# Seven block products for eight in the gate product of a quantised FFN kernel, with weight sums in natural layout and a one-step rounding

## The chip, the cores and the metric

The kernel runs on one core of one Trainium2 chip. The metric is the device time of one execution in microseconds (us), taken as the median of several runs; lower is better.

## What is computed

The reference is a cross attention followed by a quantised gated feed-forward layer, both with a residual. Cut to what matters:

```python
x = x + xattn(layernorm(x), ctx, Wq, Wkv)          # x: 2 x 2048 x 512, ctx: 2 x 128 x 512
h = act_qdq(layernorm(x))                          # rounded to multiples of one scale, 16 bits
up   = act_qdq(h @ lpbq_dequant(w_up).T)           # 512 -> 1536
gate = act_qdq(h @ lpbq_dequant(w_gate).T)         # 512 -> 1536
sig  = fixed_qdq_u16(sigmoid(gate))
gate = act_qdq(gate * sig)
o    = act_qdq(gate * up)
x = x + o @ lpbq_dequant(w_down).T                 # 1536 -> 512
```

act_qdq takes its scale from the largest absolute value of the whole tensor, so each of these steps needs a maximum over all 4096 tokens before the next can be scaled. lpbq_dequant rounds the weights to 4 bits in blocks of 32, with one scale a block.

## The kernel before

The 4096 tokens are eight groups of 512. The 1536 rows of the gate and up weights are six units of 256 a group, 48 units in all. Integers and weights are too wide for fp16, so each is held as a high and a low fp16 part, and a product of two such values is three matmuls (high x high, low x high, high x low). One unit is 2 halves x 4 slices of the 512 inputs x 3 = 24 matmuls of 128x128 on 128x512 (lines 864 to 873), and its result, 128x1024 f32, lies in two PSUM banks. Unit n takes banks 0, 1 or 2, 3 in turn, so it waits for g_ev, the copy of unit n-2 out of PSUM (line 877).

The stages follow each other, because of the maxima:

- Attention and the quantisation of the gate weights. GpSimd quantises the weights in 24 parts of 768 elements (quant_weights, lines 685 to 697): multiply by the inverse scale, add ROUND, subtract ROUND, multiply by the scale. Eight parts belong to the gate, eight to the up, eight to the down weights. GpSimd also takes each maximum across partitions (all_max, line 683).
- The gate product (L871). ScalarE copies each unit from PSUM into one of two buffers gate_out (take_gate, L993), writes its signs (L1138) and, for later groups, rounds tokens to integers (h_int, L1106). VectorE takes the unit's maximum (L1478) and splits the turned tokens into high and low (split_h, L1467, L1469). SyncE stores the unit in DRAM (gate_park, line 434), then the signs (line 436), then issues the turns (DMA transposes) of the tokens of a later group (turn_half, line 421). All DMAs of this stage stand in SyncE's one queue, in the order of the program. The order is written out by hand: a function a unit, with extra work tied to unit numbers. ScalarE's copy of unit n waits until the store of unit n-2 has landed (g_st), since both use the same gate_out.
- The up weights are loaded at line 403 and the down weights at line 443 into the same buffer WN. They are split into two fp16 parts (natural_hi, natural_lo, L1396) and turned by DMA (lines 407 and 411).
- The up product (L903), whose units rotate over four bank pairs, while ScalarE and VectorE compute the sigmoid and gate product from gate tiles that are fetched again; six gate tiles were kept on chip.
- A first pass of the down product with raw values (L929), while VectorE finds the maximum of the product o; then the down product itself (L948, L975).

In the stage of attention TensorE turns the gate weights by matmul (turn_weights), and their parts lie in WG.

## Time and profile before

| | |
|---|---|
| median of 3 runs | 902.86 us (901.2 to 903.91) |
| profiled execution: span from first to last instruction | 898.3 us |
| profiled execution: own time | not recorded apart from its span; the runs above are other executions |
| gate product, first to last matmul | 130.1 to 380.6 us |
| up product | 380.6 to 631.8 us |
| first pass of the down product | 640.0 to 726.2 us |
| down product | 728.6 to 895.1 us |

The page is one profiled execution. An engine's share says how long it had an instruction in work, and an average over stages with different limits hides which engine a stage waits for; so the stages above are read one by one. PE is TensorE, PEld its weight load, DVE VectorE, ACT ScalarE, POOL GpSimd, SPq SyncE's queue of DMA issues. PEclk is the granted clock of TensorE as a share of full speed.

### The profile page before, as it was taken

To read this page: it belongs to the slowest core of one execution; us is meant where nothing else is said; L and a number is where in the kernel's file an instruction comes from. 1 tells how busy PE (TensorE), PEld (TensorE's weight loads), DVE (VectorE), ACT (ScalarE), POOL (GpSimd) and SP (SyncE) were. 2 spreads that over 40 slices of the span, in tenths; PEclk is the share of its full clock that TensorE was granted. 3 is DMA by queue.
4 is the path that set the end of the run, shared out by engine and by line. 5 is a ranking of instruction groups with operands and counts; after the bars stand their busy time and mean duration, and the time that the engine had idled before them with its cause. 6 is when DMAs were issued, how large, how long until landed. Compare 5 with 4: busy or idle time off the path is not lost.

```text
span 898.3 us, 11791 instructions
## 1 busy us (share of the span) xinstructions
PE 865.5 (96%) x4144; PEld 426.7 (47%) x4144; DVE 651.1 (72%) x918; ACT 560.2 (62%) x673; POOL 157.4 (18%) x160
## 2 busy tenths in 40 slices
PE   7999969999999999999999989999799989999998
PEld 5777544444444444444444434444344434444443
DVE  4879883754346243279997859856999997999892
ACT  2378875553553454489997859763789975555430
POOL 0099940089001950000000000000000000000000
PEclk9999989999999999999999999999999999999999
DMA  9822319775369649884339993799998897989872
GB/s 347 332 93 98 128 59 305 205 194 198 140 234 296 206 161 294 322 319 157 132 149 327 363 347 142 251 402 373 374 379 265 276 322 271 386 286 406 317 294 100
DMA packets 107548, 230.20 MB, mean 256 GB/s; under 512 B 47216, under 2 KB 47216, under 8 KB 105328
## 3 DMA queue, kind: packets, MB, share of 16 engines
q1 hardware_dynamic: 106352, 225.48, 70.8%
q10 hardware_dynamic: 1152, 4.19, 1.3%
q8 instruction: 21, 0.34, 0.2%
q14 instruction: 23, 0.19, 0.1%
HBM read 127.40 MB, written 92.27 MB: 245 GB/s over the span
## 4 chain that ended last, share of the span: by engine, by line
PE 66%; DVE 16%; issue 8%; DMA 6%; ACT 3%; SPq 0%; POOL 0%; DVEq 0%; ACTq 0%
PE ps L871 28%; PE ps L948 13%; PE ps L903 10%; PE ps L975 3%; DVE big L1596 3%; PE ps L804 3%; DVE big L1589 3%; PE ps L743 2%; PE ps L818 2%; DVE small L1523 2%; DMA big<-gate_park 2%; DMA product_park<-big 2%; DVE small L1511 2%; DVE big L1518 1%; PE ps L965 1%
## 5 line engine op out<-in xcount | busy, mean ns | idle before, releaser
L993 ACT ACTIVATE big<-ps 128x1024 f32<-128x1024 f32 (+2 forms) x166 | 138.7, 845 | 189.6 <-PE ps L871 102.8
L871 PE MATMUL ps<-big 128*128 (+1 forms) x1152 | 250.5, 381 | 2.3 <-DVE big L1460 2.3
L903 PE MATMUL ps<-big 128*128 (+1 forms) x1152 | 249.0, 379 | 2.3 <-ACT big L993 2.3
L871 PEld LDWEIGHTS ps<-big 128*128 128x128 f16 x1152 | 113.1, 98 | 139.4 <-issue 4.6
L903 PEld LDWEIGHTS ps<-big 128*128 128x128 f16 x1152 | 112.6, 98 | 138.5 <-issue 2.8
L1478 DVE TENSOR_REDUCE small<-big 128x1 f32<-128x1024 f32 x48 | 58.3, 1219 | 135.2 <-ACT big L993 135.1
L948 PE MATMUL ps<-big 128*128 128x512 f16 x576 | 125.1, 379 | 2.7 <-DVE big L1617 2.7
L683 POOL PARTITION_ALL_REDUCE small<-small x8 | 3.3, 410 | 509.3 <-DVE small L1558 181.5
L948 PEld LDWEIGHTS ps<-big 128*128 128x128 f16 x576 | 56.2, 98 | 71.1 <-issue 2.9
L929 PE MATMUL ps<-big 128*128 128x512 f16 x384 | 85.2, 383 | 4.5 <-ACT big L1223 4.5
L1529 DVE CUSTOM_DVE_ANT_0 big<-big,small 128x1024 f32<-128x1024 int16 x48 | 61.7, 1284 | 7.3 <-ACT big L1173 0.5
L1252 ACT ACTIVATE big<-big,small 128x1024 int16<-128x1024 f32 x48 | 53.2, 1136 | 16.7 <-DMA big<-up_park 16.5
L929 PEld LDWEIGHTS ps<-big 128*128 128x128 f16 x384 | 37.4, 99 | 52.0 <-issue 5.5
L1511 DVE TENSOR_REDUCE small<-big 128x1 f32<-128x1024 f32 x48 | 58.0, 1214 | 3.4 <-ACT big L993 3.4
L1258 ACT ACTIVATE big<-big 128x1024 f16<-128x1024 int16 x24 | 25.3, 1055 | 53.0 <-DVE big L1611 53.0
L1181 ACT ACTIVATE big<-big,small 128x1024 f32<-128x1024 int16 x48 | 55.1, 1149 | 4.6 <-ACT big L1173 0.4
L1173 ACT ACTIVATE big<-big,small 128x1024 int16<-128x1024 f32 x48 | 54.5, 1136 | 2.4 <-DMA big<-gate_park 2.4
L1216 ACT ACTIVATE big<-big,small 128x1024 int16<-128x1024 f32 x48 | 52.3, 1135 | 5.7 <-DVE small L1444 2.9
L1138 ACT ACTIVATE big<-big 128x1024 int16<-128x1024 f32 x48 | 50.5, 1052 | 6.9 <-DMA sign_park<-big 5.9
L743 PE MATMUL ps<-small,big 128*128 128x128 f32 x248 | 37.9, 294 | 12.8 <-DVE big L1389 5.1
L743 PEld LDWEIGHTS ps<-small,big 128*128 128x128 f32 x248 | 32.2, 153 | 28.6 <-issue 18.4
L691 POOL TENSOR_TENSOR big<-big,small 128x768 f32<-128x768 f32 x24 | 36.5, 1521 | 22.0 <-issue 21.6
(101 smaller groups left out, 1008.9 us busy)
## 6 DMA issues: line engine op xcount, KB each, us to landing
big<-up_park SPq DMA_DIRECT2D x90, 512.0 KB, 6.5
up_park<-big SPq DMA_DIRECT2D x48, 512.0 KB, 3.9
gate_park<-big SPq DMA_DIRECT2D x42, 512.0 KB, 2.9
big<-gate_park SPq DMA_DIRECT2D x42, 512.0 KB, 5.7
sign_park<-big SPq DMA_DIRECT2D x48, 256.0 KB, 3.1
big<-in_x_dram SPq DMA_DIRECT2D x8, 1024.0 KB, 17.5
x_park<-big SPq DMA_DIRECT2D x8, 1024.0 KB, 3.9
product_park<-big SPq DMA_DIRECT2D x16, 512.0 KB, 5.8
```

The source lines that it names most:

```text
L743: return nc.tensor.transpose(dst, src, ident)
L871: mm = nc.tensor.matmul(ps[:, 2 * (n % 2) + j], w[:, a, k, o:o + P], XT[:, g, b, k], start=(k == 0 and a + b == 0), stop=(k == KC - 1 and ...
L903: mm = nc.tensor.matmul(ps[:, b + j], WU[:, a, k, o:o + P], XT[:, g, c, k], start=(k == 0 and a + c == 0), stop=(k == KC - 1 and c == 1))
L929: mm = nc.tensor.matmul(ps[:, b0 + i], halves[:, PART[t], c * 512 + i * P:c * 512 + i * P + P], WD[:, b, 2 * n + c], start=(n == 0 and c + ...
L948: mm = nc.tensor.matmul(ps[:, i], o, WD[:, b, 2 * n + c], start=(n == 0 and c + a + b == 0), stop=(n == UPG - 1 and c + a == 2))
L993: return nc.scalar.activation(dst, src, ACT.Copy)
L1173: nc.scalar.activation(g_abs[:, i % 2], place(i), ACT.Abs, scale=col["ginv"]).then_inc(abs_d, 1)
L1181: nc.scalar.activation(place(i), g_int[:, i % 2], ACT.Sigmoid, scale=col["gsc"]).then_inc(sig_d, 1)
L1252: nc.scalar.activation(r_int[:, m % 4], ring(m), ACT.Copy, scale=col["uinv"]).then_inc(uq_d, 1)
L1478: nc.vector.tensor_reduce(gcol[:, bass.ds(g * UPG + n, 1)], shelf[:, SHELF[n]] if kept else gate_out[:, n % 2], AX.X, ALU.max, apply_absol ...
L1511: nc.vector.tensor_reduce(ucol[:, n:n + 1], up_place(n), AX.X, ALU.max, apply_absolute_value=True).then_inc(u_mx, 1)
L1529: nc.vector.tensor_tensor_reduce(place(i), g_abs[:, s], s_int[:, s], 1.0, scol[:, s:s + 1], ALU.mult, ALU.max, scol[:, s:s + 1]).then_inc( ...
```

## The change

- Groups 0 to 3 (24 units, "flat") are computed as before. Groups 4, 5 and 6, 7 are two pairs. A pair and a unit of weights form a 2 x 2 by 2 x 2 block product (two halves of the weight rows, two halves of the 512 inputs, two groups), which Winograd's form of Strassen's scheme computes in seven block products for eight. Twelve such quads are left, each seven products of six matmuls (six and quad, L1027). Their sums are made from four sums of weight blocks and four sums of token blocks. Copies and differences that turn the seven products into four half tiles are done by ScalarE (copy_out, copies of 128x512) and VectorE (combine), which also takes a maximum for each half tile. All gate tiles are now stored and fetched again; none is kept.
- The weight sums are made by GpSimd from the quantised gate weights in their natural layout (weight_sums), split by ScalarE and VectorE in one buffer sum_nat (sum_hi, sum_lo), and turned by eight DMA transposes (turn_sum).
- The rounding of quant_weights is one operation for two.
- The down weights are now prepared before the up weights. They are split, turned and stored in four parts during units 10 to 20 (turn_down_weights, park_down_weights). The up weights are loaded in four column slices at units 20 and 21 (load_up_weights), in pieces of 128 elements, and turned during quads 7 to 10.
- The down weights lie in DRAM and on chip as [part, quarter of 128 outputs, input slice, 128], so each down matmul reads its moving operand in four runs of 128 (bank_of, WD[:, b, :, c]).

The diff, cut to its core:

```diff
-WTOP = 2048.0
...
+WTOP = (256.0, 2048.0, 2048.0)
+FLAT_G = 4
+FLAT = FLAT_G * UPG
+PAIRS = (NG - FLAT_G) // 2
+QUADS = PAIRS * UPG
+G_COLS = FLAT + 4 * QUADS
+SUM_AT = (2, 4, 6, 8)
+SPLIT_AT = (3, 5, 7, 9, 11, 15, 17)
+DOWN_AT = (10, 14, 15, 16)
+PARK_AT = (13, 16, 18, 20)
+TURN_AT = (18, 12)
+UP_AT = (5, 6, 7, 8)
...
+            sp.wait_ge(s_raw, S_RAW + 4)
+            sp.dma_start(WN.rearrange("p (h n) -> p h n", h=KC),
+                         wd_in.rearrange("(h p) n -> p h n", p=P)).then_inc(wn_ld[2], 16)
...
+            def turn_down_weights(e):
+                sp.wait_ge(wt_lo, OC + 3 * e + 3)
+                need(sp, wd_st, 32 * e)
+                for l in range(2):
+                    sp.dma_start(wd_turn[:, l], natural_at(2, KC - 1 - e)[:, l], transpose=True).then_inc(wd_turned, 16)
+
+            def park_down_weights(e):
+                wd_p = wd_d.rearrange("p (l h c n) -> p l h c n", l=2, h=KC, c=OC)
+                sp.wait_ge(wd_turned, 32 * e + 32)
+                for l in range(2):
+                    sp.dma_start(wd_p[:, l, KC - 1 - e], wd_turn[:, l]).then_inc(wd_st, 16)
+
+            def turn_sum(x):
+                sp.wait_ge(s_lo, S_LO + x + 1)
+                sp.wait_ge(hq_d, KC + min(x + 2, 4))
+                for l in range(2):
+                    sp.dma_start(SUMS[:, x, l].rearrange("p k n o -> p (n k) o"), sum_nat[:, l],
+                                 transpose=True).then_inc(s_turned, 16)
+
...
+            def load_up_weights(k):
+                sp.dma_start(WN.rearrange("p (k c d) -> p k c d", k=KC, c=OC)[:, k],
+                             wu_in[:, k * P:(k + 1) * P].rearrange("(c p) d -> p c d", p=P)).then_inc(up_ld[k], 16)
+
+            for u in range(FLAT):
+                sp.wait_ge(g_ev, u + 1)
+                sp.dma_start(gate_d[u], gate_out[:, u % 2]).then_inc(g_st[u % 2], 16)
+                sp.wait_ge(sign_ev, u + 1)
+                sp.dma_start(sign_d[u], sign_out[:, u % 2]).then_inc(sign_st[u % 2], 16)
+                if u < 10:
+                    turn_half(u)
+                if u - 1 in SUM_AT:
+                    turn_sum(SUM_AT.index(u - 1))
+                if u in PARK_AT:
+                    park_down_weights(PARK_AT.index(u))
+                if 13 <= u < 17:
+                    turn_half(u - 3)
+                if u + 1 in PARK_AT:
+                    turn_down_weights(PARK_AT.index(u + 1))
+                if u in (20, 21):
+                    load_up_weights(2 * u - 40)
+                    load_up_weights(2 * u - 39)
+
+            def park_half(q, x):
+                t, w = quad_tile(q, x), slice(x // 2 * 512, x // 2 * 512 + 512)
```

GpSimd and TensorE:

```diff
                 nc.gpsimd.tensor_tensor(wb, wb, inv, ALU.mult).then_inc(w_inv, 1)
-                pool.wait_ge(w_inv, base + at + 1)
-                nc.gpsimd.tensor_scalar(w, w, ROUND, 1.0, ALU.add, ALU.mult).then_inc(w_rnd, 1)
-                pool.wait_ge(w_rnd, 2 * base + 2 * at + 1)
-                nc.gpsimd.tensor_scalar(w, w, -ROUND, 1.0, ALU.add, ALU.mult).then_inc(w_rnd, 1)
-                pool.wait_ge(w_rnd, 2 * base + 2 * at + 2)
+                pool.wait_ge(w_inv, base + k + 1)
+                nc.gpsimd.tensor_scalar(w, w, ROUND, -ROUND, ALU.add, ALU.add).then_inc(w_rnd, 1)
...
                 nc.gpsimd.tensor_tensor(wb, wb, scl, ALU.mult).then_inc(w_deq, 1)
+
+            def weight_sums():
+
+                def block(r, h):
+                    return WN.rearrange("p (n r h d) -> p n r h d", n=UPG, r=2, h=2)[:, :, r, h]
+
+                s1, s2, s4, s3 = (whole_sum(x).rearrange("p (n d) -> p n d", n=UPG) for x in range(4))
+                pool.wait_ge(x2_st, 16 * NG)
+                pool.wait_ge(late_d, TI)
+                nc.gpsimd.tensor_tensor(s1, block(1, 0), block(1, 1), ALU.add).then_inc(s_raw, 1)
+                nc.gpsimd.tensor_tensor(s3, block(0, 0), block(1, 0), ALU.subtract).then_inc(s_raw, 1)
+                pool.wait_ge(s_raw, S_RAW + 1)
+                nc.gpsimd.tensor_tensor(s2, s1, block(0, 0), ALU.subtract).then_inc(s_raw, 1)
+                pool.wait_ge(s_raw, S_RAW + 3)
...
+            def six(bank, n, w, x, begin):
+                for k in range(2):
+                    for a, b in ((0, 0), (1, 0), (0, 1)):
+                        mm = nc.tensor.matmul(ps[:, bank], w[:, a, k, n], x[:, b, k],
+                                              start=(begin and k + a + b == 0), stop=(k + b == 2), skip_group_check=True)
+                mm.then_inc(q_mm, 1)
...
+            def quad(q):
+                base, pr, n = 4 * ((q + 1) % 2), q // UPG, q % UPG
+                g, T = pair_group(pr), turns(pr)
+                need(pe, c_ev, C_EV + 4 * (q - 1) if q > 1 else 0)
+                if q == 1:
+                    pe.wait_ge(g_ev, FLAT)
+                six(base, n, block(0), XT[:, g, :, 0:2], True)
+                if n == 0:
+                    pe.wait_ge(s_turned, S_TURNED + 128)
+                    pe.wait_ge(t_lo, T_LO + 4 * PAIRS)
+                six(base + 3, n, SUMS[:, 0], T[:, 0], True)
+                six(base + 2, n, block(2), T[:, 3], True)
+                pe.wait_ge(c_ev, C_EV + 4 * q + 1)
+                six(base, n, SUMS[:, 1], T[:, 2], False)
+                pe.wait_ge(copy_ev, COPY_EV + 4 * q + 2)
+                six(base + 3, n, SUMS[:, 2], XT[:, g + 1, :, 2:4], False)
+                if q == 0:
+                    pe.wait_ge(g_ev, FLAT - 1)
+                if q + 1 < QUADS:
+                    first_of(q + 1, 4 - base)
+                pe.wait_ge(copy_ev, COPY_EV + 4 * q + 4)
+                six(base, n, SUMS[:, 3], T[:, 1], False)
 
...
-                                mm = nc.tensor.matmul(ps[:, b0 + i], halves[:, PART[t], c * 512 + i * P:c * 512 + i * P + P],
-                                                      WD[:, b, 2 * n + c], start=(n == 0 and c + b == 0),
+                                mm = nc.tensor.matmul(bank_of(b0 + i), halves[:, PART[t], c * 512 + i * P:c * 512 + i * P + P],
+                                                      WD[:, b, :, 2 * n + c], start=(n == 0 and c + b == 0),
                                                       stop=(n == UPG - 1 and c + b == 2))
```

ScalarE and VectorE:

```diff
+            def sum_hi(x):
+                act.wait_ge(s_raw, S_RAW + 4)
+                if x:
+                    act.wait_ge(s_turned, S_TURNED + 32 * x)
+                nc.scalar.activation(sum_nat[:, 0], whole_sum(x), ACT.Copy,
+                                     scale=1.0 if x == 2 else 4.0).then_inc(s_hi, 1)
...
+            for u in range(FLAT):
+                act.wait_ge(g_mm, u + 1)
+                need(act, g_mx, u - 1)
+                if u >= 2:
+                    act.wait_ge(g_st[u % 2], 16 * (u // 2))
+                copy(gate_out[:, u % 2], ps[:, 2 * (u % 2):2 * (u % 2) + 2].rearrange("p b w -> p (b w)")).then_inc(g_ev, 1)
+                if u % 2 and u < 2 * NG - 3:
+                    h_int((u + 3) // 2)
+                if u in SUM_AT:
+                    sum_hi(SUM_AT.index(u))
+                for pr in range(PAIRS):
+                    for j in range(4):
...
+                nc.scalar.activation(sign_out[:, u % 2], gate_out[:, u % 2], ACT.Sign).then_inc(sign_ev, 1)
...
+            def combine(q, x, bank, other, op):
+                if q:
+                    dve.wait_ge(c_st[x], C_ST + 16 * q)
+                    dve.wait_ge(c_sign, C_SIGN + 4 * (q - 1) + x + 1)
+                else:
+                    dve.wait_ge(g_st[x // 2], 16 * FLAT // 2)
+                    dve.wait_ge(sign_ev, FLAT)
+                    dve.wait_ge(g_mx, FLAT)
+                nc.vector.tensor_tensor(gate_half[:, x], ps[:, bank], other, op).then_inc(c_ev, 1)
...
+            def turn_raw(pr, j):
+
+                g = pair_group(pr)
+                first = (ints(g + 1, 0), ints(g + 1, 1), raw_sum[:, 1], raw_sum[:, 0])[j]
+                second = (ints(g, 0), ints(g + 1, 0), ints(g, 0), ints(g, 1))[j]
+                if j > 1:
+                    dve.wait_ge(t_raw, T_RAW + (j if pr else 4 + j))
+                    dve.wait_ge(t_lo, T_LO + (j - 1 if pr else 4 + j - 1))
+                elif pr == 0:
+                    dve.wait_ge(t_lo, T_LO + 4)
+                else:
+                    dve.wait_ge(s_turned, S_TURNED + 128)
+                nc.vector.tensor_tensor(raw_sum[:, j % 2], first, second,
+                                        ALU.add if j == 2 else ALU.subtract).then_inc(t_raw, 1)
+
+            def turn_lo(pr, j):
```

Three places in the order of instructions. First SyncE's queue at the start of the gate product. Before, the load of the up weights, then units 0 and 1 (gate_park and sign_park are the stores of a unit, 128x4x128 the token turns):

```order
L403 DMA big<-in_L_ffn_w_up_dram 128x12x512 [waits wt_lo]
L434 DMA gate_park<-big 128x1024 [waits g_ev]
L436 DMA sign_park<-big 128x1024 [waits sign_ev]
L421 DMA_TRANSPOSE big<-big 128x4x128 [waits hq_d]
L421 DMA_TRANSPOSE big<-big 128x4x128
L434 DMA gate_park<-big 128x1024 [waits g_ev]
```

Now (h2_d is the semaphore that counts the weight sums here):

```order
L473 DMA big<-in_L_ffn_w_down_dram 128x4x1536 [waits h2_d,wt_lo]
L519 DMA gate_park<-big 128x1024 [waits g_ev]
L521 DMA sign_park<-big 128x1024 [waits sign_ev]
L510 DMA_TRANSPOSE big<-big 128x4x128 [waits hq_d]
L510 DMA_TRANSPOSE big<-big 128x4x128
L519 DMA gate_park<-big 128x1024 [waits g_ev]
```

The load at the head of the queue waits for one thing more, and the stores of all units stand behind it.

Second, ScalarE around units 2 to 4 (L1177 the copy of a unit, L1263 the high part of a weight sum, L1338 the signs, L1308 the token rounding; wg_ld1 counts turned weight sums):

```order
L1177 ACTIVATE big<-ps 128x1024 [waits g_st0,g_mx,g_mm]
L1263 ACTIVATE big<-big 128x1536 [waits h2_d]
L1338 ACTIVATE big<-big 128x1024 [waits sign_st0,g_ev]
L1177 ACTIVATE big<-ps 128x1024 [waits g_st1,g_mx,g_mm]
L1308 ACTIVATE big<-big,small 128x2048 [waits wq_ld]
L1338 ACTIVATE big<-big 128x1024 [waits sign_st1,g_ev]
L1177 ACTIVATE big<-ps 128x1024 [waits g_st0,g_mx,g_mm]
L1263 ACTIVATE big<-big 128x1536 [waits wg_ld1,h2_d]
```

The rows L1263 are new; from the second on each waits for a DMA transpose that SyncE issues in unit 3 and later:

```order
L519 DMA gate_park<-big 128x1024 [waits g_ev]
L521 DMA sign_park<-big 128x1024 [waits sign_ev]
L510 DMA_TRANSPOSE big<-big 128x4x128 x2
L498 DMA_TRANSPOSE big<-big 128x12x128 [waits hq_d,ve1_d]
L498 DMA_TRANSPOSE big<-big 128x12x128
L519 DMA gate_park<-big 128x1024 [waits g_ev]
```

That is unit 3 and the start of unit 4 in SyncE's queue; the two rows L498 (turn_sum) stand between them.

Third, GpSimd between the scale of the tokens and the quantisation of the next weights:

```order
L806 ISA small<-small 128x1 [waits col_max]
L829 ISA
L829 TENSOR_TENSOR big<-big 128x1536 [waits late_d,x2_st]
L830 TENSOR_TENSOR big<-big 128x1536
L832 TENSOR_TENSOR big<-big 128x1536 [waits h2_d]
L834 TENSOR_TENSOR big<-big 128x1536 [waits h2_d]
L806 ISA
```

L806 is the maximum across partitions; the four sums are new and stand right behind it.

## Rows read from the trace of the kernel before

**Rows 1.** The page, busy us of each engine (share of the span) xinstructions

```profile
PE 865.5 (96%) x4144; PEld 426.7 (47%) x4144; DVE 651.1 (72%) x918; ACT 560.2 (62%) x673; POOL 157.4 (18%) x160
```

**Rows 2.** Groups by line: shapes xcount | busy us, mean ns | idle before, releaser

```profile
L871 PE MATMUL ps<-big 128*128 (+1 forms) x1152 | 250.5, 381 | 2.3 <-DVE big L1460 2.3
L903 PE MATMUL ps<-big 128*128 (+1 forms) x1152 | 249.0, 379 | 2.3 <-ACT big L993 2.3
L948 PE MATMUL ps<-big 128*128 128x512 f16 x576 | 125.1, 379 | 2.7 <-DVE big L1617 2.7
```

**Rows 3.** Timeline of ScalarE, early gate units: start, us, engine line op [idle, releaser]

```profile
147.84 1.02 ACT L993 ACTIVATE big<-ps 128x1024 f32<-128x1024 f32 x1 [1.60 <-DMA gate_park<-big]
...
152.75 1.02 ACT L993 ACTIVATE big<-ps 128x1024 f32<-128x1024 f32 x1 [2.79 <-PE ps L871]
...
168.29 1.02 ACT L993 ACTIVATE big<-ps 128x1024 f32<-128x1024 f32 x1 [1.32 <-PE ps L871]
169.34 1.06 ACT L1138 ACTIVATE big<-big 128x1024 int16<-128x1024 f32 x1
173.47 1.02 ACT L993 ACTIVATE big<-ps 128x1024 f32<-128x1024 f32 x1 [3.07 <-PE ps L871]
174.39 1.99 ACT L1106 ACTIVATE big<-big,small 128x2048 int16<-128x2048 f32 x1
```

**Rows 4.** Stretches: us, busy PE, PEld, DVE, ACT, POOL (xcount), PEclk, DMA share, GB/s

```profile
333.00:356.00 23.00, 23.00 (x108) 10.47 (x107) 8.87 (x11) 11.21 (x14) 0.00 (x0) 1.00 1.06 249
356.00:368.00 12.00, 12.00 (x58) 5.40 (x56) 3.66 (x3) 5.19 (x5) 0.00 (x0) 1.00 1.02 388
534.00:538.00 4.00, 2.03 (x10) 0.71 (x8) 2.85 (x5) 3.91 (x4) 0.00 (x0) 1.00 0.98 376
640.00:642.00 2.00, 2.00 (x5) 0.67 (x6) 1.97 (x4) 2.00 (x3) 0.00 (x0) 0.50 1.01 396
644.00:650.00 6.00, 6.00 (x30) 2.68 (x28) 5.93 (x8) 5.09 (x6) 0.00 (x0) 1.00 1.05 400
650.00:680.00 30.00, 29.63 (x137) 13.08 (x135) 29.73 (x34) 26.74 (x27) 0.00 (x0) 1.00 0.96 367
```

**Rows 5.** Timeline of GpSimd and VectorE around two reductions and the quantisation behind one

```profile
125.43 0.17 DVE L1449 TENSOR_REDUCE small<-small 128x1 f32<-128x18 f32 x1
127.25 0.38 POOL L683 PARTITION_ALL_REDUCE small<-small  x1 [5.78 <-issue]
...
175.88 0.35 POOL L683 PARTITION_ALL_REDUCE small<-small  x1 [48.25 <-DVE small L1312]
183.05 1.47 POOL L691 TENSOR_TENSOR big<-big,small 128x768 f32<-128x768 f32 x1 [6.82 <-issue]
184.61 0.83 POOL L693 TENSOR_SCALAR big<-big 128x768 f32<-128x768 f32 x1
...
L1324 DVE TENSOR_SCALAR small<-small x2: 320/320/321, 176.8 to 280.9; 128x192 f32<-128x192 f32 x2
```

**Rows 6.** SyncE's issues, and the time to landing by line (min/median/max)

```profile
135.00 0.41 SPq L403 DMA_DIRECT2D big<-in_L_ffn_w_up_dram  x1
138.26 0.35 SPq L434 DMA_DIRECT2D gate_park<-big  x1
...
160.75 2.87 SPq L421 DMA_TRANSPOSE big<-big  x2
...
L403 SPq DMA_DIRECT2D big<-in_L_ffn_w_up_dram x1: 407/407/407, 135.0 to 135.0; - x1
DMA to landing us min/median/max: 11.4/11.4/11.4
...
L411 SPq DMA_TRANSPOSE big<-big x8: 1485/1994/2884, 333.2 to 352.3; - x8
DMA to landing us min/median/max: 4.0/4.7/5.3
...
L421 SPq DMA_TRANSPOSE big<-big x28: 1229/1266/3969, 139.7 to 208.3; - x28
DMA to landing us min/median/max: 2.5/2.8/9.4
```

**Rows 7.** VectorE's split of tokens, without and with GpSimd at work

```profile
155.66 1.23 DVE L1469 TENSOR_TENSOR big<-big 128x2048 f16<-128x2048 int16 x1
...
186.45 1.80 POOL L697 TENSOR_TENSOR big<-big,small 128x768 f32<-128x768 f32 x1
186.94 2.38 DVE L1469 TENSOR_TENSOR big<-big 128x2048 f16<-128x2048 int16 x1
```

**Rows 8.** Groups by line, of the shapes that the quads use

```profile
L1361 DVE SCALAR_TENSOR_TENSOR big<-ps,small,big 128x512 f32<-128x512 f32 x32 | 23.9, 746 | 6.8 <-PE ps L818 6.5
L993 ACT ACTIVATE big<-ps 128x512 f32<-128x512 f32 x56 | 32.7, 596 | 38.9 <-PE ps L743 21.7 <-PE ps L780 5.7 <-PE ps L761 5.7
L1478 DVE TENSOR_REDUCE small<-big 128x1 f32<-128x1024 f32 x48 | 58.3, 1219 | 135.2 <-ACT big L993 135.1
```

**Rows 9.** Timeline of TensorE behind two idle times

```profile
538.32 6.86 PE L903 MATMUL ps<-big 128*128 x31 [2.29 <-ACT big L993]
...
639.96 39.72 PE L929 MATMUL ps<-big 128*128 128x512 f16 x176 [3.52 <-ACT big L1223]
```

**Rows 10.** Timeline of the first up units

```profile
380.47 39.88 PE L903 MATMUL ps<-big 128*128 128x512 f16 x184
...
391.51 1.00 ACT L993 ACTIVATE big<-ps 128x1024 f32<-128x1024 f32 x1
```

More of the change, by code:

```diff
@@ L468, in _ @@
[L468 to L479 removed]
+                                 transpose=True).then_inc(h_turn[g % 2], 16)
@@ L892, in _ @@
             gate(0)
-            with nc.tensor.Fori(1, NG) as g:
+            with nc.tensor.Fori(1, FLAT_G) as g:
                 gate(g)
-            pe.wait_ge(wu_turned, 16 * (2 * KC + H_ODD))
+            for g in range(FLAT_G, NG):
+                pe.wait_ge(hlo_d, g + KC)
+            first_of(0, 4)
+            for q in range(QUADS):
+                quad(q)
+            pe.wait_ge(wu_turned, 16 * 2 * KC)
             def raise_unit(g, n):
@@ L1150, in take_up @@
+            half_sign(QUADS - 1, 2)
+            half_sign(QUADS - 1, 3)
             def take_up(n):
```

545 lines of the change are left out of this document (346 added, 199 removed).

## The prediction

> **What bounds the kernel now.** I read the page's busy shares first [rows 1], then the groups by line [rows 2], then stretches of time. TensorE is busy 96% of the 898.3 us span. The gate product (L871) is 1152 matmuls that cover 250.50 us without a gap after the first. The steady pace is the distance between two evictions, 173.47 - 168.29 = 5.18 us for a unit of 24 matmuls [rows 3], so 0.216 us a matmul. The up product (L903) has 2.3 us of idle, and the down product is TensorE too. Only 632 to 725 us belongs to VectorE: it is busy 29.73 of 30 us there [rows 4]. So a matmul taken out of the gate product is worth its full time, as long as nobody makes TensorE wait. The question is therefore the cover: TensorE writes unit u+2 over the banks of unit u, so ScalarE's copy of unit u may end as late as the end of unit u+1, 5.18 us after unit u itself, and no later. ScalarE copies a unit only when SyncE's store of unit u-2 has landed, and every store, turn and load stands in SyncE's one queue.
>
> **The change, part by part.** Sums are made against the profiled execution (span 898.3 us); the median of the runs, 902.86, is 4.6 us above it, and I carry that over unchanged.
>
> *Matmuls.* Twelve quads of 7 x 6 replace twelve of 48: 72 matmuls fewer, 72 x 0.216 = **-15.5 us**.
>
> *Rounding in one operation.* It takes one operation of 0.83 us off each of 24 parts [rows 5]. Only the last ones before the gate lie near a path: the reduction that gives the scale of h starts at 127.25, when GpSimd has been without other work for 5.78 us, and VectorE had its input ready 1.6 us before. I take **-0.6** (0 to -1.6).
>
> *Weight sums, and the load behind them.* After a reduction GpSimd begins elementwise work only after 6.8 us, although the scales it needs were ready at 177.1 [rows 5]. The sums come after such a reduction: 127.63 + 6.9 = 134.5. Four sums of 1536 elements at twice 1.48 us, 2.96 each, end at 146.4. The load of the next weights now waits for them (L473), and it stands in SyncE's queue *ahead of* the first gate store. Before, it left at 135.00, and the store of unit 0 behind it landed at 147.84, 12.8 us later, the one DMA wait of that stretch [rows 3, 6]. Now: 146.4 + 12.8 = 159.2, copy of unit 2 done at 160.2, TensorE wants those banks at 152.7. **+7.5** (2, if the store overtakes the load, to 9).
>
> *The turns of the sums.* sum_nat has one buffer: ScalarE makes sum x+1 (units 2, 4, 6, 8) only after the turns of sum x have landed, and SyncE issues those behind the sign store and the token turns of the next unit. Round: sum copy 1.5 (between 1.05 for 1024 and 1.99 for 2048 elements), sign 1.06, copy 1.02, token rounding 1.99, sign 1.06 [rows 3], sign store 0.33, two token turns 2.8, two weight turns of which the second leaves at +2.0 and lands 4.7 later [rows 6]: 16.5 us, where two units last 10.4. Three rounds are 18.3 late, and ScalarE may be 4.2 late before TensorE feels it: 14; the first stall has used part of the same time, so I take **+12** (6 to 14; at the token turns' 1.27 and 2.8 the round would be 13.8, and three of them 6 late).
>
> *Units 12 to 23.* SyncE waits inside its queue for each pair of down turns to land before it parks them. A round with token turns is 1.4 for four stores, 5.6, 4.0, 2.7 and 0.7: 14.4 for 10.4. That hits once or twice, 4 to 8. VectorE's new two-input operations meet GpSimd's quantisation there: the same TENSOR_TENSOR took 1.23 alone and 2.38 beside GpSimd's [rows 7]. **+8** (0 to 16). The Trainium skill has this as a lock ("SBUF — State Buffer", Who interferes with whom): a VectorE instruction with two SBUF inputs blocks against GpSimd reading SBUF, one with a PSUM input does not. By that rule, and the trace agrees, the combines of the quads pay nothing.
>
> *The switch to quads.* The first combine waits for every gate store. From the last down turns on, the DMA queue has about 4 + 2 (park) + 8 (3 MB of up weights; 3 MB landed in 11.4 us [rows 6]) + 8 (four stores and signs) = 22 us of work for 15.5 us of units; TensorE's cover is four products, 5.2 us. On time that is a stall of 1; with the lateness above, **+7** (1 to 15). The upper end is for the 512-byte pieces in which these weights are now read: the nearest rows are turns, 249 GB/s against 388 GB/s for whole rows [rows 4]. By the Trainium skill ("DMA: Bandwidth & Descriptors", Specifications) 512 bytes is still line rate, which would leave the load at its old length; no row here shows it.
>
> *Inside the quads.* VectorE needs 4 x 0.75 + 4 x 0.61 = 5.4 us and ScalarE 4.8 of 9.1, from the 512-element rows and half of a 1024 maximum [rows 8]; block maxima (quads 0, 1) and low parts beside GpSimd (quads 5, 6) overrun now and then: **+1.5** (0 to 5).
>
> *The clock.* After 2.29 us of idle the granted clock stayed full, after 3.52 us it was at half, 1.2 GHz, for the first 2 us and back at full, 2.4 GHz, four us on [rows 4, 9]. As at the gate's start, that costs 1.7 us. Where a later stall is set by ScalarE anyway the loss is swallowed; I count four: **+6.8** (0 to 10).
>
> *Up and down product.* The first copy of an up unit came at 391.51, 8.7 us before TensorE needed it (four units after 380.47) [rows 10], which covers six more fetches; the down weights are read back in pieces, the first pass starts only when they and the first tiles are there: **+1** (0 to 3). The down product's moving operand becomes four runs of 128 instead of one of 512. No matmul of the trace has that shape; With nothing for or against it I take 0, the price of today's row (379 ns shown, 0.216 us of pace [rows 2]), and keep the other end as a rival.
>
> Sum: -15.5 - 0.6 + 7.5 + 12 + 8 + 7 + 1.5 + 6.8 + 1 = +27.7, **930.6 us**.
>
> **Rivals.**
> 1. *The cover holds* (ends faster). One mechanism: transfers of the queue overlap so well that turns land like the token turns, 1.27 and 2.8 us. Then the store of unit 0 lands in time (2), the round is 13.8 us and three cost 6, the switch costs 1, the quads 1, units 12 to 23 and the clock nothing: -16.1 + 10 = -6.1, 896.8 us. For it: SyncE hid 16 such turns without a stall. Against: there nothing waited for them inside a unit. It decides where all stalls together are under 16 us. 0.12.
> 2. *Near no change*: half of my stalls, 0.05, about 903.
> 3. *Everything late*: up weights at half speed (+8), units 12 to 23 and quads at their upper ends (+9): 947 us. 0.2.
> 4. *Strided reads cost*: 1152 matmuls of the down product a tenth slower, 25 us (at twice the time nothing else would matter), with the main case 955 us. 0.05.
> 5. That the change doesn't do what it says: the order lists 504 block matmuls and one rounding, so only the rounding could be dear; at 1.7 us it gives back what the two took. Inside the others.
>
> **Numbers.** Main case 0.58, its own range 915 to 942. The predicted time is its sum, 930.6. The range takes the main case, most of case 3, and down to no change: 902 to 950. A measurement of this kernel tells about 0.3%, 2.7 us. Slower 0.82, same 0.06, faster 0.12.
>
> **What would show it.** In the profile after: GpSimd's four sums at 134 to 147 and the weight load issued at their end; ScalarE's copy of unit 2 waiting for gate_park near 158; sum copies 16 us apart that wait for a DMA; TensorE idle some 30 us within the flat units and at the sixth product of quad 0, none of it in quads 2 to 11, whose pace is 9.1 us; down matmuls at 0.216. I am wrong if the sums' copies are 10.4 apart, if unit 2 is copied before 152, or if the gate stretch (380.6 - 130.1 = 250.5 us before) is shorter than 250.

## The result, and the profile after

| | kernel before | changed kernel |
|---|---|---|
| median | 903.2 us (4 runs) | 947.02 us (946.68 to 947.82, 4 runs) |
| ratio to before | | 1.0489, 95% interval 1.0471 to 1.0507 |
| profiled execution, span | 898.3 us | 945.3 us (own time 947.09 us) |
| TensorE busy | 96% [rows 1] | 92% |

The change makes the kernel 44 us slower. The forecast had 930.6 us: the sign is right and the time lies in the range on record, the size is 16 us short. The page of the changed kernel answers to [rows 1], the groups by line (line engine op names shapes xcount, busy us, mean ns, idle before it and its releasers) to [rows 2]:

```profile
PE 873.0 (92%) x4072; PEld 427.4 (45%) x4072; DVE 718.1 (76%) x1016; ACT 578.8 (61%) x733; POOL 202.2 (21%) x140
L1011 PE MATMUL ps<-big 128*128 (+1 forms) x576 | 136.2, 402 | 30.1 <-ACT big L1177 28.1 <-DVE big L1693 2.1
L1027 PE MATMUL ps<-big 128*128 128x512 f16 x504 | 111.1, 384 | 8.6 <-DVE big L1780 8.6
L1082 PE MATMUL ps<-big 128*128 (+1 forms) x1152 | 251.9, 383 | 3.2 <-ACT big L1177 3.2
L1132 PE MATMUL ps<-big 128*128 128x512 f16 x576 | 126.7, 383 | 2.4 <-DVE big L1940 2.4
L817 POOL TENSOR_SCALAR big<-big 128x768 f32<-128x768 f32 x24 | 71.4, 2974 | 2.1
```

L1011 is the flat units, L1027 the quads, L1082 the up product, L1132 the down product (L948 before), L817 the rounding. The 72 matmuls are gone, and TensorE has 28.0 us of idle inside the flat units (30.1 less the 2.1 ahead of the first) and 8.6 in quad 0. The page shows one thing that was not in the forecast: one rounding takes 2.97 us where two took 0.83 each [rows 5].

To see where the time lies, the span is cut at the first matmul of each stage. The stretches of before (columns: us, busy us of PE, PEld, DVE, ACT, POOL with counts, granted clock, DMA share, GB/s) are gate product, up product, first pass, down product and end:

```profile
130.10:380.50 250.40, 250.36 (x1153) 113.19 (x1154) 110.94 (x113) 124.90 (x131) 79.04 (x66) 0.99 0.73 227
380.50:640.00 259.50, 251.23 (x1178) 114.68 (x1177) 206.77 (x294) 201.00 (x192) 1.08 (x3) 1.00 0.74 273
640.00:728.60 88.60, 85.19 (x384) 37.35 (x385) 87.36 (x105) 79.60 (x78) 0.71 (x1) 0.98 0.88 315
728.60:898.30 169.70, 166.08 (x768) 74.99 (x768) 143.96 (x144) 73.74 (x71) 0.00 (x0) 1.00 0.80 299
```

and of the changed kernel, with the gate product in two rows, flat units and quads:

```profile
138.80:302.90 164.10, 136.03 (x576) 58.33 (x577) 98.90 (x92) 81.50 (x83) 67.08 (x29) 0.91 0.73 203
302.90:422.40 119.50, 110.93 (x505) 49.67 (x504) 78.06 (x116) 62.48 (x108) 47.86 (x25) 0.96 0.73 222
422.40:685.70 263.30, 254.18 (x1177) 115.25 (x1175) 208.02 (x298) 200.25 (x193) 1.08 (x3) 0.99 0.81 293
685.70:774.40 88.70, 85.26 (x385) 37.64 (x386) 87.46 (x105) 79.82 (x79) 0.72 (x1) 0.98 0.92 319
774.40:945.30 170.90, 167.60 (x768) 75.38 (x768) 144.00 (x144) 73.60 (x71) 0.00 (x0) 0.99 0.79 297
```

The start is 8.7 us later (138.8 for 130.1), the gate product 33.2 us longer (283.6 for 250.4), the up stage 3.8, the last two 0.1 and 1.2: 47.0 in all.

**The start.** The timeline of GpSimd (start us, us, engine line op, idle before it and releaser), which answers to [rows 5]:

```profile
116.60 2.79 POOL L817 TENSOR_SCALAR big<-big 128x768 f32<-128x768 f32 x1
...
135.90 0.38 POOL L806 PARTITION_ALL_REDUCE small<-small  x1 [5.89 <-issue]
143.01 3.42 POOL L829 TENSOR_TENSOR big<-big 128x1536 f32<-128x1536 f32 x1 [6.74 <-issue]
```

The reduction that gives the scale of h starts 8.65 us after its 127.25 of before. Each of the eight parts of the gate weights takes 1.0 us more (4.9 us before, 5.9 now, with its gaps), and GpSimd is what the setup now waits for, which the first experiment shows. The sums begin 6.7 us behind the reduction, as forecast, and take 3.42 us each for the 2.96 that I had scaled.

**The flat units.** SyncE's queue behind the sums, and ScalarE's copy of unit 2, which answers to the first of [rows 3]:

```profile
156.82 0.41 SPq L473 DMA_DIRECT2D big<-in_L_ffn_w_down_dram  x1
157.28 0.50 SPq L519 DMA_DIRECT2D gate_park<-big  x1
...
158.30 9.11 SPq L510 DMA_TRANSPOSE big<-big  x2
...
169.82 1.02 ACT L1177 ACTIVATE big<-ps 128x1024 f32<-128x1024 f32 x1 [14.94 <-DMA gate_park<-big]
170.74 1.48 ACT L1263 ACTIVATE big<-big 128x1536 f16<-128x1536 f32 x1
```

The store of unit 0 leaves behind the load at 157.28 and lands 12.5 us later. The later copies of sums (L1263) stand at 187.37, 202.62 and 217.89, each after a wait of 8.2 to 8.5 us for the turns of the sum before: rounds of 16.6, 15.3 and 15.3 us, forecast 16.5. TensorE's timeline at five of its eight idle times:

```profile
170.90 17.29 PE L1011 MATMUL ps<-big 128*128 128x512 f16 x72 [9.55 <-ACT big L1177]
190.77 12.22 PE L1011 MATMUL ps<-big 128*128 x48 [2.58 <-ACT big L1177]
206.02 10.53 PE L1011 MATMUL ps<-big 128*128 x48 [3.03 <-ACT big L1177]
...
265.17 17.93 PE L1011 MATMUL ps<-big 128*128 x72 [5.16 <-ACT big L1177]
...
316.83 8.42 PE L1027 MATMUL ps<-big 128*128 128x512 f16 x29 [8.57 <-DVE big L1780]
```

The first stall is 9.55 us, the three of the sums' rounds 2.58 + 3.03 + 4.73 = 10.3, units 12 to 23 0.42 + 5.16 + 2.58 = 8.2, the switch 8.57, and in the quads behind it there is none.

### The profile page after: what moved, and what is told of

It reads as the page before. It is cut to its first block, busy times and chain, and to the rows that moved or that the text cites. A ratio compares the mean times of both kernels' runs of the same rounds, so it can differ in the third digit from the quotient of the medians.

```text
span 945.3 us, 11963 instructions
## 1 busy us (share of the span) xinstructions
PE 873.0 (92%) x4072; PEld 427.4 (45%) x4072; DVE 718.1 (76%) x1016; ACT 578.8 (61%) x733; POOL 202.2 (21%) x140
## 4 chain that ended last, share of the span: by engine, by line
PE 40%; issue 18%; DMA 11%; DVE 11%; POOL 10%; SPq 5%; ACT 3%; DVEq 0%; POOLq 0%; ACTq 0%
PE ps L1132 13%; PE ps L1027 11%; PE ps L1082 10%; PE ps L1159 3%; DMA big<-big 3%; SPq L510 3%; POOL big L817 2%; POOL big L844 2%; DMA big<-in_L_ffn_w_gate_dram 2%; DMA big<-gate_park 2%; DMA gate_park<-big 2%; DVE small L1834 2%; DVE small L1845 2%; DMA product_park<-big 2%; DVE big L1727 1%
## 5 line engine op out<-in xcount | busy, mean ns | idle before, releaser
L1082 PE MATMUL ps<-big 128*128 (+1 forms) x1152 | 251.9, 383 | 3.2 <-ACT big L1177 3.2
L1177 ACT ACTIVATE big<-ps 128x1024 f32<-128x1024 f32 (+2 forms) x142 | 113.8, 813 | 119.9 <-DMA gate_park<-big 32.6
L1082 PEld LDWEIGHTS ps<-big 128*128 128x128 f16 x1152 | 113.2, 98 | 141.7 <-issue 7.5
L1011 PE MATMUL ps<-big 128*128 (+1 forms) x576 | 136.2, 402 | 30.1 <-ACT big L1177 28.1
L1132 PE MATMUL ps<-big 128*128 128x512 f16 x576 | 126.7, 383 | 2.4 <-DVE big L1940 2.4
L1027 PE MATMUL ps<-big 128*128 128x512 f16 x504 | 111.1, 384 | 8.6 <-DVE big L1780 8.6
L806 POOL PARTITION_ALL_REDUCE small<-small x8 | 3.3, 414 | 493.0 <-DVE small L1881 181.8
L1011 PEld LDWEIGHTS ps<-big 128*128 128x128 f16 x576 | 58.3, 102 | 107.9 <-ACT big L1177 26.0
L1113 PE MATMUL ps<-big 128*128 128x512 f16 x384 | 85.2, 385 | 4.5 <-ACT big L1450 4.5
L1132 PEld LDWEIGHTS ps<-big 128*128 128x128 f16 x576 | 56.7, 98 | 71.9 <-issue 5.1
L1027 PEld LDWEIGHTS ps<-big 128*128 128x128 f16 x504 | 49.7, 99 | 69.8 <-DVE big L1780 9.1
L817 POOL TENSOR_SCALAR big<-big 128x768 f32<-128x768 f32 x24 | 71.4, 2974 | 2.1
L1738 DVE TENSOR_REDUCE small<-big 128x1 f32<-128x1024 f32 x24 | 29.2, 1215 | 42.0 <-ACT big L1177 41.5
L1113 PEld LDWEIGHTS ps<-big 128*128 128x128 f16 x384 | 37.6, 99 | 51.8 <-issue 6.0
L1834 DVE TENSOR_REDUCE small<-big 128x1 f32<-128x1024 f32 x48 | 58.0, 1214 | 3.0 <-ACT big L1177 2.9
L1780 DVE TENSOR_TENSOR big<-ps,big 128x512 f32<-128x512 f32 x48 | 31.6, 686 | 26.6 <-PE ps L1027 22.0
```

The source lines that it names most:

```text
L817: nc.gpsimd.tensor_scalar(w, w, ROUND, -ROUND, ALU.add, ALU.add).then_inc(w_rnd, 1)
L1011: mm = nc.tensor.matmul(ps[:, 2 * (n % 2) + j], WG[:, x, a, k % 2, o:o + P], XT[:, g, b, k], start=(k == 0 and a + b == 0), stop=(k == KC ...
L1027: mm = nc.tensor.matmul(ps[:, bank], w[:, a, k, n], x[:, b, k], start=(begin and k + a + b == 0), stop=(k + b == 2), skip_group_check=True)
L1082: mm = nc.tensor.matmul(ps[:, b + j], WU[:, a, k, o:o + P], XT[:, g, c, k], start=(k == 0 and a + c == 0), stop=(k == KC - 1 and c == 1))
L1113: mm = nc.tensor.matmul(bank_of(b0 + i), halves[:, PART[t], c * 512 + i * P:c * 512 + i * P + P], WD[:, b, :, 2 * n + c], start=(n == 0 an ...
L1132: mm = nc.tensor.matmul(bank_of(i), o, WD[:, b, :, 2 * n + c], start=(n == 0 and c + a + b == 0), stop=(n == UPG - 1 and c + a == 2))
```

## The experiments

Every ratio is to the kernel before on the same chip in the same session, with its 95% interval. Theory A and rival B stand in each text on record.

### Two roundings again

```diff
-                nc.gpsimd.tensor_scalar(w, w, ROUND, -ROUND, ALU.add, ALU.add).then_inc(w_rnd, 1)
+                nc.gpsimd.tensor_scalar(w, w, ROUND, 1.0, ALU.add, ALU.mult).then_inc(w_rnd, 1)
+                pool.wait_ge(w_rnd, 2 * base + 2 * k + 1)
+                nc.gpsimd.tensor_scalar(w, w, -ROUND, 1.0, ALU.add, ALU.mult).then_inc(w_rnd, 1)
```

> Changed kernel with the rounding of the weights put back into two GpSimd operations. Theory A: one operation that adds twice takes 2.79 us where two that add once and multiply by one took 0.83 each, so every part lost 1.1 us, and GpSimd became the engine that sets the start of the gate product. Then the gate product starts at 130.1 instead of 138.8, and the parts of the down weights, 8 x 1.1 us earlier, take 0 to 4 us from units 12 to 17: 934 to 938 us. Rival B: the start was late for another reason (order of the queue, stores) and the long operation lies beside other work: start at 138 to 139, 945 to 947 us.

Measured: 941.33 us, ratio 1.0427 (1.0400 to 1.0453), 5.7 us less than the changed kernel. The gate product starts at 130.8, as A has it, but its stretch is 287.0 us for 283.6: the first stall is 10.37 us and the second half of the flat units stalls no less. So the start was GpSimd's, but 3.4 of the 8.0 us are lost again behind it, and the down weights' shorter parts bring nothing there; the time is above A's 934 to 938.

### The one-operation rounding alone, in the kernel before

> Kernel before with the one-operation rounding alone. Theory A: gate product starts 8.6 us later, 911 to 915 us. Rival B: nothing but a shorter or equal setup, 902 to 903 us.

Measured: 918.12 us, ratio 1.0164 (1.0143 to 1.0185): 15.6 us, more than A had. Alone it costs as much as a third of the whole loss of 44 us, though taking it out of the changed kernel gave back only 5.7. GpSimd's group by line, TensorE's and ScalarE's timelines:

```profile
L693 POOL TENSOR_SCALAR big<-big 128x768 f32<-128x768 f32 x24 | 68.0, 2833 | 2.1
...
138.15 27.10 PE L869 MATMUL ps<-big 128*128 128x512 f16 x117 [2.10 <-DVE big L1458]
...
342.63 1.67 ACT L991 ACTIVATE big<-big 128x512 f16<-128x512 f32 x3 [9.91 <-POOL big L695]
...
346.21 19.13 PE L869 MATMUL ps<-big 128*128 x80 [4.20 <-ACT big L991]
```

8.0 us are the start. Then ScalarE, which takes part of the down weights between two copies, waits 9.91 us for GpSimd's late part and TensorE 4.20 for ScalarE; with the clock the gate stretch is 6.9 us longer. I had looked for the price at the start only. B is excluded.

### Is it the two additions?

```diff
-                nc.gpsimd.tensor_scalar(w, w, ROUND, 1.0, ALU.add, ALU.mult).then_inc(w_rnd, 1)
...
-                nc.gpsimd.tensor_scalar(w, w, -ROUND, 1.0, ALU.add, ALU.mult).then_inc(w_rnd, 1)
+                nc.gpsimd.tensor_scalar(w, w, ROUND, ROUND, ALU.add, ALU.subtract).then_inc(w_rnd, 1)
```

> Kernel before with one rounding operation that adds and then subtracts (the changed kernel's adds and then adds the negative). Theory A: what is dear is a second operation that is no multiplication; it takes 2.8 us again and the time is that of the run with two additions, 915 to 920 us. Rival B: only two additions in one operation are dear; add and subtract takes 0.83 us, GpSimd saves 0.9 us a part, and the time is that of before or up to 1 us less: 901 to 904 us.

Measured: 918.83 us, ratio 1.0193 (1.0143 to 1.0244). The group by line:

```profile
L693 POOL TENSOR_SCALAR big<-big 128x768 f32<-128x768 f32 x24 | 68.0, 2834 | 2.1
```

The same 2.83 us as two additions: A holds for both forms that were tried. Add and then multiply takes 0.83 at this shape [rows 5]. Other second operations were not tried.

### The load of the down weights behind unit 1

The wait for the sums and the load move from ahead of the loop over the flat units to behind `turn_half(u)` of unit 1.

> Changed kernel with the wait for the weight sums and the load of the down weights moved in SyncE's queue from ahead of the first gate store to behind the stores and turns of unit 1. Theory A: the first stall (9.55 us, and 1.7 us of half clock behind it) is the store of unit 0 that is queued behind a wait for GpSimd and a 3 MB load; both go, 936 us. Rival B: the load is only met by the next stores: the store of unit 2 leaves behind the load and lands some 12 us later, near 169.5, when TensorE wants the banks of unit 4 at 170; part of the stall comes back one or two units later, 940 to 947 us.

Measured: 940.36 us, ratio 1.0412 (1.0386 to 1.0437), 6.7 us less: between A and B. The first stall is gone, and 4 us of it are met again: 2.9 in the first round of the sums and 1.2 at the switch to the quads (9.80 us for 8.57). SyncE's queue, ScalarE and TensorE in this run:

```profile
157.85 0.51 SPq L522 DMA_DIRECT2D big<-in_L_ffn_w_down_dram  x1
...
159.86 7.26 SPq L505 DMA_TRANSPOSE big<-big  x2
...
170.68 1.02 ACT L1177 ACTIVATE big<-ps 128x1024 f32<-128x1024 f32 x1 [5.51 <-DMA gate_park<-big]
...
182.68 12.68 PE L1011 MATMUL ps<-big 128*128 x48 [5.49 <-ACT big L1177]
```

Behind the load the queue needs 7.26 us to issue the two turns of a unit (2.5 to 3 without it; [rows 6] have 1.27 for one). The copy of unit 4 comes at 170.68, just in time, but the first round of the sums starts late and its stall is 5.49 us where it was 2.58.

### Sums in their own buffers

```diff
+        def sum_nat_of(x):
+            start = (U0 + 4096, 3 * 2048, U0 + 4096, 5 * 2048)[x]
...
-                if x:
-                    act.wait_ge(s_turned, S_TURNED + 32 * x)
+                if x == 2:
+                    act.wait_ge(s_turned, S_TURNED + 32)
+                if x == 3:
+                    act.wait_ge(s_lo, S_LO + 2)
```

with waits in `split_h` of groups 3 and 5, which take that space over.

> Changed kernel in which the halves of sum 1 and sum 3 are written over token groups of X that are free then (3 and 5), so that no copy of a sum waits for the turns of the sum before. Theory A: the one buffer is what makes the rounds 15.3 to 16.6 us; its three stalls (10.3 us) and the half clock behind each (3 x 1.7 us) go: 932 us. Rival B: the round is the queue's own work (three pairs of turns at 2.9, 2.9 and 3.3 us and four stores, 11 us of issue for two units of 10.4), so stores are late anyway: rounds of 12 to 15 us, 938 to 946 us.

Measured: 939.09 us, ratio 1.0408 (1.0382 to 1.0435), 7.9 us less. ScalarE's timeline:

```profile
179.57 1.48 ACT L1271 ACTIVATE big<-big 128x1536 f16<-128x1536 f32 x1
...
190.80 1.48 ACT L1271 ACTIVATE big<-big 128x1536 f16<-128x1536 f32 x1
...
201.03 1.02 ACT L1183 ACTIVATE big<-ps 128x1024 f32<-128x1024 f32 x1 [2.74 <-DMA gate_park<-big]
```

The three stalls of the rounds are gone, so the single buffer made them. But copies of sums are 11.2 us apart where two units last 10.4, and the wait is now for a gate store: the queue's own work, B's number. The lateness returns as 0.45 + 1.02 + 1.38 + 2.39 + 1.45 us of stalls from 215 to 248 us. Each theory has half of it.

### The up weights behind the last gate store

`load_up_weights` of all four pieces moves from units 20 and 21 to behind the loop; their block maxima from quads 0 and 1 to 1 and 2.

> Changed kernel with the four loads of the up weights moved in SyncE's queue from units 20 and 21 to behind the last store of the flat units, and their block maxima from quads 0 and 1 to quads 1 and 2. Theory A: the stall of 8.57 us at the sixth product of quad 0 is the last gate stores, queued behind 3 MB of loads in 512-byte pieces; it falls to 1 to 3 us and half clock with it: 937 to 940 us. Rival B: the stores are late by themselves (signs, copies and the turns ahead of them), or VectorE now waits for the weights inside quads 1 and 2 and TensorE with it: 944 to 950 us.

Measured: 943.16 us, ratio 1.0445 (1.0413 to 1.0477), 3.9 us less, between A and B. SyncE and VectorE, and a stretch in which the loads are what the DMA engines mostly move (columns as above):

```profile
305.82 6.87 SPq L514 DMA_DIRECT2D big<-in_L_ffn_w_up_dram  x4
312.73 2.64 SPq L539 DMA_DIRECT2D gate_park<-big  x1
...
319.98 0.69 DVE L1780 TENSOR_TENSOR big<-ps,big 128x512 f32<-128x512 f32 x1 [5.02 <-DMA gate_park<-big]
...
310.00:318.00 8.00, 7.52 (x35) 3.23 (x33) 2.67 (x4) 3.37 (x6) 0.00 (x0) 1.00 1.19 290
```

The 8.57 us at quad 0 are gone; in their place the first half store of quad 0 is queued behind 6.87 us of issuing the loads, which stalls quad 1 by 3.2 us. A later quad stalls by 1.7 us, whose cause I did not follow. The loads in 512-byte pieces move at 290 GB/s with the DMA engines fully busy (share 1.19), where whole rows have 388 in [rows 4]: about three quarters of the rate.

### Weight sums on VectorE

> Changed kernel with the four weight sums made by VectorE instead of GpSimd. Theory A: GpSimd's 6.7 us after its reduction and its 3.42 us a sum are what holds back the load of the down weights and with it the store of unit 0; VectorE takes 1.9 us a sum (1.21 to 1.24 us for 1024 elements), ends at 150 instead of 156.8, and 6 to 7 of the first stall of 9.55 us go: 939 to 941 us. Rival B: VectorE, busy until 151, is late with the maxima of units 0 and 1 and the first split, and TensorE waits for that instead: 944 to 950 us.

Measured: 939.12 us, ratio 1.0395 (1.0352 to 1.0439), 7.9 us less, A's number. TensorE's first stall is

```profile
164.18 1.25 PE L995 MATMUL ps<-big 128*128 128x512 f16 x3 [2.27 <-ACT big L1161]
```

2.27 us for 9.55. Of the others most stay (2.57, 3.05; 4.47, 3.06); one falls from 4.73 to 1.78, and the switch rises from 8.57 to 10.04.

### Mended together

> Two roundings, load behind unit 1 and sums in their own buffers together (alone: 5.7, 6.7 and 7.9 us less than the changed kernel). Theory A: they mend separate places and add up: 927 us. Rival B: the lateness is shared (SyncE's queue needs about 12.3 us for two units with a turned sum, 10.4 us are there), so that a stall taken away in one place comes back in the next: 931 to 936 us. No theory has it under the kernel before.

Measured: 925.27 us, ratio 1.0244 (1.0209 to 1.0279). Three gains of 5.7, 6.7 and 7.9 us make 20.3, and 21.7 were measured: they add up, A. That fits with what each alone lost again to a stall that another one mends (3.4 us behind the earlier start, 2.9 in the first round behind the moved load). All five do not add up: 32 us alone, 26 together in the next run.

> All of it: two roundings, sums on VectorE, load behind unit 1, sums in their own buffers, up weights loaded behind the flat stores. Theory A: with each wait mended only units 11 to 20 stall (VectorE beside GpSimd), 8 to 12 us: 905 to 912 us. Rival B: queue and engines have no room for the added work, 915 to 925 us. All stalls gone would be 888 to 890 us.

Measured: 921.14 us, ratio 1.0186 (1.0150 to 1.0222): B. The gate product starts at 130.6 and lasts 264.8 us, still 14.4 more than before. In the flat units there are seven stalls of 1.2 to 3.8 us, 17.8 in all, and 5.2 us in the quads.

### What holds units 10 to 17: VectorE beside GpSimd

In the run with all mended, GpSimd's rounding of the down weights works on one block of 32 elements of each part.

> The run with all mended, with GpSimd's rounding of the down weights left out but for one block of each part (this work is left out, the down weights stay unrounded). Theory A: in units 10 to 17 VectorE's operations take 1.8 to 1.9 us instead of 1.2 because GpSimd reads SBUF beside them; without it they return to 1.2, the stalls of units 11 to 16 (2.6, 3.0 and 3.8 us, with half clock) go: 909 to 913 us. Rival B: the stalls there are the queue's and ScalarE's order, and only the operations get shorter: 918 to 921 us.

Measured: 911.98 us, ratio 1.0095 (1.0063 to 1.0127), 9 us less (8 by the ratios): A's time. Of the three stalls that A names, those of 2.6 and 3.0 us are gone, and the one of 3.8 is still 3.6. VectorE's groups between 205 and 235 us, with the rounding beside it and then without:

```profile
L1744 DVE SCALAR_TENSOR_TENSOR big<-big 128x1024 f16<-128x1024 f32 x4 | 7.6, 1932 | 0.0
L1749 DVE TENSOR_REDUCE small<-big 128x1 f32<-128x1024 f32 x4 | 4.8, 1205 | 0.0
L1738 DVE TENSOR_TENSOR big<-big 128x1024 f32<-128x1024 f32 x2 | 3.6, 1782 | 0.0
```

```profile
L1751 DVE TENSOR_REDUCE small<-big 128x1 f32<-128x1024 f32 x4 | 4.9, 1214 | 1.2 <-ACT big L1171 1.2
L1746 DVE SCALAR_TENSOR_TENSOR big<-big 128x1024 f16<-128x1024 f32 x4 | 4.7, 1215 | 0.0
L1740 DVE TENSOR_TENSOR big<-big 128x1024 f32<-128x1024 f32 x2 | 2.4, 1220 | 0.0
```

The operations with two SBUF inputs go from 1.93 and 1.78 to 1.22 us, the reduction with one input stays at 1.21. The Trainium skill ("SBUF — State Buffer", Who interferes with whom) has this as a lock between VectorE with two SBUF inputs and GpSimd; the trace agrees, and it adds the size: half as long again for these two, and more for others of the same stretch (TENSOR_TENSOR 128x512: 1.67 us, then 0.69). In the run with all mended no engine waits for GpSimd itself between 200 and 245 us, so it is not that the down weights came late. Stalls of 3.6 and 3.0 us are left behind that stretch, so not all of it is the lock.

### Sums further apart, signs first, and the down weights later

```diff
-SUM_AT = (2, 4, 6, 8)
+SUM_AT = (2, 5, 8, 10)
```

and in ScalarE's loop the sign of unit u stands ahead of `h_int`, `sum_hi`, `turn_hi` and `natural_hi`. A third thing differs from the run with all mended: only the last of the four sums has a buffer of its own (over token group 6), and the other three share one again.

> The run with all mended, and in it the turned sums three units apart (units 2, 5, 8, 10) and ScalarE's sign of a unit ahead of its extra work in that unit. Theory A: in units 4 to 11 the stalls (1.2, 2.3 and 1.8 us) are SyncE's queue, 12.3 us of work for two units; spread over three units they go, and the store of a unit no longer waits for a sign behind ScalarE's waits for VectorE: 911 to 916 us. Rival B: ScalarE's waits for VectorE set units 11 to 20 whatever the order, and signs ahead make VectorE's inputs later: 918 to 922 us. Neither has it under the kernel before.

Measured: 907.90 us (10 runs), ratio 1.0061 (1.0036 to 1.0085): 13 us less than with all mended (11 by the ratios), more than A had. Of the three stalls that A names (TensorE met them ahead of units 10, 12 and 14) one of 1.8 us is left, ahead of unit 13; the last one, of 3.0 us, is gone too. The flat units last 142.0 us for 148.4. The edits were not tried apart.

In the last run the down weights are halved and turned later and the up loads stand one by one between the half stores:

```diff
-DOWN_AT = (10, 14, 15, 16)
-PARK_AT = (13, 16, 18, 20)
+DOWN_AT = (14, 16, 19, 20)
+PARK_AT = (16, 18, 21, 23)
```

> The run with spaced sums, and in it the halving and the turns of the down weights moved from units 10, 14, 15 and 16 to 14, 16, 19 and 20 (parks to 16, 18, 21 and 23), since VectorE is busy from 196 to 242 us and has room behind 258, and the four up loads put one by one between the half stores of quads 0 and 1. Theory A: VectorE's overfull stretch is what still stalls units 10 to 16 (1.8, 2.5, 3.0 and 3.4 us) and the four loads in a row the switch (3.2 us): 8 to 10 us of stalls and two or three cold starts go: 895 to 900 us, under the kernel before. Rival B: the work is only met later: the splits of units 14 to 17 already fill VectorE and queue, and down turns and parks now meet the last gate stores: 903 to 908 us.

Measured: 900.37 us (12 runs) against 902.95 (17 runs), ratio 0.9987 (0.9972 to 1.0002). That is 0.4 us above A's range, and the interval holds 1: no difference from the kernel before is shown. The stretches, and the wait that takes back what the gate product wins:

```profile
130.60:261.60 131.00, 125.00 (x576) 55.87 (x577) 110.02 (x96) 84.42 (x83) 54.23 (x33) 1.00 0.86 244
261.60:376.30 114.70, 109.63 (x505) 48.93 (x504) 83.33 (x116) 61.85 (x108) 39.59 (x33) 1.00 0.81 243
376.30:639.40 263.10, 253.54 (x1178) 115.68 (x1177) 208.22 (x298) 200.49 (x193) 1.09 (x3) 0.99 0.81 294
...
529.34 1.15 ACT L1391 ACTIVATE big<-big,small 128x1024 int16<-128x1024 f32 x1 [8.15 <-DMA big<-gate_park]
...
536.12 9.11 PE L1077 MATMUL ps<-big 128*128 x34 [4.24 <-ACT big L1172]
```

The gate product lasts 245.7 us, 4.7 less than before: 15.5 of matmuls won, 6.0 and 5.1 us of idle paid. The up stage is 3.6 us longer. Its wait for a gate fetch (7.11 us in the same place before) is 8.15, its stall 4.24 where [rows 9] have 2.29, and this one is followed by half clock. The same stage is longer in every run with block products, and 2.7 us longer in the kernel before with the one rounding, whose stall there is 3.3; why was not settled.

## Why the prediction was right or wrong

The range of 902 to 950 us held, but not by the main case: its own range ended at 942, and 947 is inside only because the range took in most of rival 3, whose reasons were not the ones found. That it held is in part luck. Of the 19.3 us that the sum missed, 9.3 are the rounding, 5.3 the clock and 4.1 the up and down product.

By its own steps, against the profiled execution (forecast +27.7, found +47.0):

| step | forecast | found |
|---|---|---|
| matmuls | -15.5 | -15.5 |
| rounding in one operation | -0.6 | +8.7 |
| first stall | +7.5 | +9.6 |
| turns of the sums | +12 | +10.3 |
| units 12 to 23 | +8 | +8.2 |
| switch to quads | +7 | +8.6 |
| inside quads | +1.5 | 0 |
| clock | +6.8 | +12.1 |
| up and down product | +1 | +5.1 |

*Matmuls*: right. 474 matmuls behind the switch take 104.48 us in the chain of waits; less 1.7 of half clock that is 0.217 each.

*Rounding*: the step that failed. I wrote "it takes one operation of 0.83 us off each of 24 parts", taking the price of an operation from its shape (128x768) although its pair of operations was another. No row of before had two additions, so it was an unknown cost to be bounded from both sides, and I bounded it above at 0 (0 to -1.6); only in the last rival did I price it, at 1.7, which still gave nothing. It is 2.8 (3.0 in the mean of the changed kernel, single ones up to 3.6). That this sets the start is shown: with two roundings 8.0 of the 8.7 us go. And I looked only at "the last ones before the gate": the run with this edit alone pays 15.6 us, nearly half of it far behind the start.

*First stall*: right in place and mechanism (load behind the sums, store behind the load; both runs that take this away mend it). 2.1 us short, since the sums take 3.42 each and not 2.96; the landing was forecast at 12.8 and is 12.5.

*Turns of the sums*: right in mechanism, shown by the run with own buffers, and nearly in size. The rounds after the first are 15.3 and not 16.5. What I did not see is that the queue alone needs 11.2.

*Units 12 to 23*: 8.2 for 8. Lock and order both seem to have a part: held against the run with all mended, the one without the down rounding gains 8 to 9 us and the one with sums apart and signs first 11 to 13, part of it here. In the changed kernel itself they were not separated.

*Switch and quads*: 8.6 for 7, and right that it is the up loads: with them moved the stall of quad 0 is gone. In the quads, nothing: my 1.5 was not needed.

*Clock*: I counted four times 1.7. Found: 283.6 us less 1080 x 0.216 = 233.3, less 28.0 and 8.6 of idle, leaves 13.7, of which the kernel before had 1.6. There were seven idle times over 2.5 us, and half clock followed six of them: those stretches are 1.6 to 2.2 us longer than as many matmuls at full clock (12.22 for 10.53 us in 48), 11 us in all. The one behind 3.03 us ran at full clock. The last 1.2 us are the ends of the stretches: 10.53 us for 48 matmuls and 31.25 for 144 make 0.17 us an end, and there are seven more of them. My row for a pause without half clock, 534 to 538 us in [rows 4], ends before TensorE resumes; the reading holds all the same, since the clock was full from 538.3 to 540.3 us.

*Up and down*: I gave the up stage 1 us for its copies and left out that its old stall of 2.29 us could grow past what the clock bears. It is 3.18, and the 432 matmuls behind it take 96.3 us where they took 93.4; half clock also met the down product's start (1.2 us net). Together 5.1.

*Rivals.* "The cover holds" is out, as are strided reads (down matmuls 379 to 383 ns, 31.24 us for 144 in both kernels; the down stretch grows by its cold start alone). "Everything late" gives 947 us, the number found, but for other reasons. Its up weights at half speed did not show, but neither do they land in the old time, which the prediction also weighed: 290 GB/s for 388, and 13.2 us from the first issue to the last landing in the run with the loads moved, where the one load of 3 MB took 11.4 [rows 6].

## What to carry to other kernels

Price an instruction by its form, not only by its shape and engine: a fused one has to be found in a trace, or bounded from above by the sum of what it replaces and more. Work taken off a bound engine is worth its time only if the transfers and small operations that it costs find room in queues; here the queue's issue time (about 1 us for the two stores of a unit, 2.5 to 3 for a pair of token turns, 3.3 for a pair of sum turns) against the time of two units, 10.4 us, told that a sum turned every second unit does not fit. And a stall that is mended alone comes back in part at the next one; three mended together gave the sum of the three and a little more.
